# Routing in one 512-column product per block: the high and the low part of a transposed block side by side, their sum taken on VectorE

## The reference, cut to what matters

```python
W = weights[condition]                                   # 64 matrices of 128x128, chosen per batch
h = jnp.einsum('bct,bcd->bdt', x, W)                     # x is 64 x 128 x 2048
flat = h.reshape(T, H)                                   # one token: 2048 numbers
logits = jnp.einsum('th,eh->te', flat, router_weight) + router_bias     # 64 experts
scores = jax.nn.softmax(logits, axis=-1)
topk_w, topk_idx = jax.lax.top_k(scores, 8)
w_sum = topk_w.sum(axis=-1, keepdims=True)
bias_mix = jnp.einsum('te,eh->th', w_dense, expert_bias) # w_dense: topk_w at topk_idx, else 0
out = x + (flat * w_sum + bias_mix).reshape(...)
```

## Time and profile before

| | |
|---|---|
| median of 3 runs | 559.57 us (558.46 to 559.75) |
| the profiled execution | 558.69 us, of which its instructions span 556.9 us |
| TensorE busy | 541.0 us, 97% of the span |
| VectorE busy | 471.2 us, 85% |
| ScalarE busy | 368.5 us, 66% |
| GpSimd busy | 354.4 us, 64% |
| mean granted TensorE clock | 0.993 |

### The profile page before, as it was taken

How to read it: one execution, slowest core, us unless ns; L and a number is a source line. 1 busy time by engine, 2 the same in 40 slices (tenths; PEclk the granted TensorE clock), 3 DMA queues, 4 the chain that set the end, 5 groups by cost and what they waited for, 6 DMA issues and landing times.

```text
span 556.9 us, 12892 instructions
## 1 busy us (share of the span) xinstructions
PE 541.0 (97%) x3360; PEld 477.0 (86%) x3360; DVE 471.2 (85%) x1055; ACT 368.5 (66%) x836; POOL 354.4 (64%) x326
## 2 busy tenths in 40 slices
PE   5879999999999999999999999999999999999997
PEld 5768888888888888888888888888888888888875
DVE  2488898988889988889988889898888998888975
ACT  3576666677666677666677666667666667766661
POOL 0176666766666776666776666676666677666676
PEclk9979999999999999999999999999999999999999
DMA  8986999888999888898888999888899888889245
GB/s 243 311 201 231 309 297 279 292 300 287 297 318 276 269 311 289 295 325 280 292 276 296 294 311 300 271 290 297 286 298 315 284 283 295 288 294 326 119 166 212
DMA packets 70850, 155.96 MB, mean 280 GB/s; under 512 B 6322, under 2 KB 45234, under 8 KB 62770
## 3 DMA queue, kind: packets, MB, share of 16 engines
q1 hardware_dynamic: 70834, 155.77, 85.6%
HBM read 88.64 MB, written 67.11 MB: 280 GB/s over the span
## 4 chain that ended last, share of the span: by engine, by line
PE 93%; DMA 3%; SPq 1%; ACT 1%; issue 1%; DVE 1%; ACTq 0%; DVEq 0%
PE zt_ps L337 21%; PE xt_ps L325 14%; PE p_ps L390 11%; PE p_ps L387 11%; PE p_ps L385 11%; PE p_ps L386 10%; PE p_ps L391 10%; PE scores_ps L360 2%; DMA out_sb<-L_ffn_expert_bias 2%; PE scores_ps L369 1%; PE scores_ps L351 1%; DMA cond_sb<-itok_B 1%; SPq L243 0%; SPq L244 0%; DVE xt_lo L546 0%
## 5 line engine op out<-in xcount | busy, mean ns | idle before, releaser
L681 POOL TENSOR_TENSOR x_lo<-x_sb,x_hi 128x512 fp32r<-128x512 f32 x256 | 327.0, 1308 | 176.2 <-ACT x_hi L459 176.2
L546 DVE TENSOR_TENSOR xt_lo<-xt_ps,xt_hi 128x512 fp32r<-128x512 f32 x256 | 175.7, 687 | 63.6 <-ACT xt_hi L451 60.8
L451 ACT CAST xt_hi<-xt_ps 128x512 fp32r<-128x512 f32 x256 | 148.2, 582 | 102.9 <-PE xt_ps L325 84.9
L612 DVE SCALAR_TENSOR_TENSOR out_sb<-p_ps,w_sum,x_sb 128x512 f32<-128x512 f32 x256 | 189.6, 740 | 6.2 <-PE p_ps L391 6.2
L459 ACT CAST x_hi<-x_sb 128x1024 fp32r<-128x1024 f32 x128 | 133.7, 1045 | 0.5 <-PE p_ps L391 0.5
L337 PE MATMUL zt_ps<-xt_hi,router_hl 128*128 128x256 f32 x512 | 129.6, 285 | 4.5 <-DVE xt_lo L546 4.5
L337 PE MATMUL zt_ps<-xt_lo,router_hl 128*128 128x256 f32 x512 | 129.2, 285 | 0.0
L325 PE MATMUL xt_ps<-ident,x_sb 128*128 128x128 f32 x784 | 119.2, 277 | 0.1
L385 PE MATMUL p_ps<-x_hi,w_hl 128*128 128x512 f32 x256 | 118.8, 464 | 0.0
L337 PEld LDWEIGHTS zt_ps<-xt_hi,router_hl 128*128 128x128 f32 x512 | 98.1, 192 | 11.0 <-DVE xt_lo L546 5.2
L337 PEld LDWEIGHTS zt_ps<-xt_lo,router_hl 128*128 128x128 f32 x512 | 98.4, 192 | 4.8
(11 more groups left out here) (38 smaller groups left out, 368.7 us busy)
## 6 DMA issues: line engine op xcount, KB each, us to landing
out<-out_sb SPq DMA_DIRECT2D x126, 512.0 KB, 4.2
x_sb<-x SPq DMA_DIRECT2D x62, 1024.0 KB, 6.8
x_turn<-x SPq DMA_DIRECT2D x120, 128.0 KB, 4.7
w_sb<-L_cond_weights SPq DMA_DIRECT2D x64, 64.0 KB, 5.3
x_sb<-x SPq DMA_DIRECT2D x4, 256.0 KB, 6.0
x_sb<-x SPq DMA_DIRECT2D x2, 512.0 KB, 8.0
out_sb<-L_ffn_expert_bias SPq DMA_DIRECT2D x2, 512.0 KB, 9.4
out<-out_sb SPq DMA_DIRECT2D x4, 256.0 KB, 2.5
```

Of the source, the lines that this page charges most:

```text
L451: act.copy(xt_hi[:, n % 2, :, r, :], xt_ps[v % 4][:, :].rearrange("p (q c) -> p q c", c=P)).then_inc(xt_hi_ready, 1)
L546: dve.tensor_tensor(xt_lo[:, n % 2, :, r, :], xt_ps[v % 4][:, :].rearrange("p (q c) -> p q c", c=P), xt_hi[:, n % 2, :, r, :].bitcast(F32) ...
L612: dve.scalar_tensor_tensor(out_sb[:, r, cols], p_ps[n % 2][:, :], w_sum[:, o % 2, r:r + 1], x_sb[:, (2 * o + r) % XRING, cols], ALU.mult, ...
L681: pool.tensor_tensor(x_lo[:, r, cols], x_sb[:, (2 * o + r) % XRING, cols], x_hi[:, r, cols].bitcast(F32), ALU.subtract).then_inc(x_lo_read ...
```

## The change

`xt_hi` and `xt_lo` become one tile `xt_hl`, in which each block of 256 rounded columns is followed by its 256 columns of rests. `route` makes one product of 512 columns for each block, which fills the whole bank `zt_ps`: the sum over the rounded part stands in the first half, that over the rests in the second. ScalarE copies the first half to a new tile `zt_of_hi` in slot 1, and VectorE adds the second half to it (`zt_sum`, new, slot 1). `turn_z` moves from slot 1 to slot 2, and `z_sum` from slot 2 to slot 3. `score` stays where it was.

```diff
@@ route, TensorE
-                    for xt in (xt_hi, xt_lo):
-                        last = pe.matmul(zt_ps[:, 0:2 * P],
-                                         router_hl[:, t, :, :].rearrange("p a e -> p (a e)"),
-                                         xt[:, n % 2, q, :, :].rearrange("p r c -> p (r c)"),
-                                         start=(t == 0 and xt is xt_hi),
-                                         stop=(t == TB - 1 and xt is xt_lo))
+                    last = pe.matmul(zt_ps[:, :], router_hl[:, t, :, :].rearrange("p a e -> p (a e)"),
+                                     xt_hl[:, n % 2, q, :, :, :].rearrange("p h r c -> p (h r c)"),
+                                     start=(t == 0), stop=(t == TB - 1))
@@ step, TensorE
-                    if mid and v == 1:
+                    if mid and v == 2:
                         turn_z(m, i - 1)
@@ zt_copy, ScalarE
-                act.copy(zt_sb[:, :, :], zt_ps[:, 0:2 * P].rearrange("p (r c) -> p r c", r=2)).then_inc(zt_ready, 1)
+                wait(act, zt_ready, i)
+                act.copy(zt_of_hi[:, :, :],
+                         zt_ps[:, 0:2 * P].rearrange("p (r c) -> p r c", r=2)).then_inc(zt_of_hi_ready, 1)
@@ VectorE
+            def zt_sum(m, o):
+                i = 4 * m + o
+                dve.wait_ge(zt_of_hi_ready, i + 1)
+                dve.tensor_tensor(zt_sb[:, :, :], zt_ps[:, 2 * P:4 * P].rearrange("p (r c) -> p r c", r=2),
+                                  zt_of_hi[:, :, :], ALU.add).then_inc(zt_ready, 1)
@@ step, VectorE
-                    if mid and v == 2:
+                    if mid and v == 1:
+                        zt_sum(m, i - 1)
+                    if mid and v == 3:
                         z_sum(m, i - 1)
```

More of the change, by code:

```diff
@@ L90, in adaln_router @@
         w_hl = sb("w_hl", [P, 8, 2, D], F32R)
-        xt_hi = sb("xt_hi", [P, 2, BLOCKS, 2, P], F32R)
-        xt_lo = sb("xt_lo", [P, 2, BLOCKS, 2, P], F32R)
+        xt_hl = sb("xt_hl", [P, 2, BLOCKS, 2, 2, P], F32R)
         kept_t_hi = sb("kept_t_hi", [P, 2, 2, P], F32R)
@@ L97, in adaln_router @@
         w_sum = sb("w_sum", [P, 2, 2])
+        zt_of_hi = sb("zt_of_hi", [P, 2, P])
         zt_sb = sb("zt_sb", [P, 2, P])
@@ L158, in adaln_router @@
         w_hl_ready = sem("w_hl_ready")
+        zt_of_hi_ready = sem("zt_of_hi_ready")
         zt_ready = sem("zt_ready")
@@ L450, in xt_high @@
                 wait(act, routed, PIECES * i + n - 1)
-                act.copy(xt_hi[:, n % 2, :, r, :],
+                act.copy(xt_hl[:, n % 2, :, 0, r, :],
                          xt_ps[v % 4][:, :].rearrange("p (q c) -> p q c", c=P)).then_inc(xt_hi_ready, 1)
@@ L545, in xt_low @@
                 dve.wait_ge(xt_hi_ready, SLOTS * (4 * m + o) + v + 1)
-                dve.tensor_tensor(xt_lo[:, n % 2, :, r, :], xt_ps[v % 4][:, :].rearrange("p (q c) -> p q c", c=P),
-                                  xt_hi[:, n % 2, :, r, :].bitcast(F32), ALU.subtract).then_inc(xt_lo_ready, 1)
+                dve.tensor_tensor(xt_hl[:, n % 2, :, 1, r, :], xt_ps[v % 4][:, :].rearrange("p (q c) -> p q c", c=P),
+                                  xt_hl[:, n % 2, :, 0, r, :].bitcast(F32), ALU.subtract).then_inc(xt_lo_ready, 1)
             def relay(m, o, v):
```

## The result

| | before | after |
|---|---|---|
| median | 559.66 us (4 runs, 558.46 to 560.89) | 595.52 us (4 runs, 595.20 to 596.06) |
| ratio of the runs | 1 | 1.0642, 95% interval 1.0617 to 1.0666 |
| profiled execution | 558.69 us, span 556.9 | 595.20 us, span 593.3 |

The change makes the kernel 6.4% slower. The forecast was 592.1 us with a range of 585 to 598.

A forecast was written before the change was run, and what follows sets the result against it. TensorE, 97% busy, was taken as the bound. Each of 30 full steps loses 1.23 us at `score` less 0.11 gained, 33.6 us; remaining routing gives back 0.2, so 33.4 on 558.69 makes 592.1 us, range 585 to 598.

The forecast's parts named there:

- What bounds the kernel: Whole kernel: TensorE is full, busy 97% of the span; what one of 30 full steps gains or loses counts thirty times.
- The products: Routing on TensorE: 512-column products save 0.028 us a `route` call, 0.11 us a full step, 3.6 us in all.
- The addition: VectorE, slot 1: `zt_sum` pushes back what follows by 0.33 us, at most 0.41; TensorE doesn't wait for it at `turn_z`.
- z_sum and the wait at score: `z_sum` ends 1.58 us later against a margin of 0.54, so TensorE loses 1.23 us at `score` each full step.
- 0.06 us from the end of a VectorE operation to the product that it releases: Term of the loss at `score`: release delay of 0.06 us, read between `xt_low` and a product in the start.
- 0.10 us for the first product after a wait: Term of the loss at `score`: a first product after a wait takes 0.10 us more, 0.38 against 0.28.
- The start: Step 1: first scores may come about 1 us later, but a 3.61 us TensorE wait at 31.32 covers that.
- VectorE's addition costs the stretch nothing: Rival, VectorE's busy stretch: the addition fits into an unseen gap, 0.33 us leaves each wait, 582 us; chance 0.06.
- No wait: Rival at `score`: `z_sum` is in time, only the shorter routing is left, 555.1 us, faster; chance 0.05.
- The clock falls: Rival on TensorE: pauses each step lower its clock, costing 33 us, 625 us or more; chance 0.05, shared with another second wait.
- back-to-back issue gap: Skill page's rule for TensorE products, N/2.4 + 2.5 ns: products would gain 1.3 us, whole sum 2.3 us higher.

The follow-up runs named there:

- the first experiment: The changed kernel with `z_sum` alone put back to slot 2 on VectorE: 559.41 us, ratio 0.9991 to the kernel before.

## Why the prediction was right

**What bounds the kernel: right.** TensorE had no slack, and each wait in the loop came through in full; the table above has it at three delays.

**The products: right.** Forecast 0.028 us for a call of `route`, 0.11 us in a step and 3.6 us in all. Measured 0.13 us in a period and 3.6 to 4 us with the products alone.

**The addition: right.** 0.33 us from its start to the next one, 306.64 to 306.97. `turn_z` in slot 2 does not wait for it in the full steps.

**z_sum and the wait at score: right in place and nearly in size.** Forecast 1.23 us of loss at `score`, measured 1.30; three small terms were off. Shown by taking it away (one line moved back: 595.5 to 559.4) and by making it alone (1.0503 without products and addition). The term "0.06 us from the end of a VectorE operation to the product that it releases" was too small: it is 0.15 us at `score`, in each full step here and in all the kernels with a hold, and the missing 0.09 us is more than the 0.05 that the range allowed for distances. I had read it off a routing product; why that one starts sooner is not shown. The time doesn't go by the engine or the kind of product alone, as the last section has it. The term "0.10 us for the first product after a wait" is 0.08 here. The savings that stand against them were 0.13 and not 0.11. These misses partly cancel: +0.09, -0.02 and -0.02 make the 0.05 us by which the period, forecast as 17.65, is longer at 17.70.

**The start: wrong.** "TensorE waits 3.61 us a little behind them, which covers that" did not hold. Here are the waits of TensorE in the start of the changed kernel:

```profile
22.44 0.44 PE L349 MATMUL scores_ps<-ident,zt_sb 128*128 128x128 f32 x2 [1.25 <-DVE zt_sb L563]
25.18 0.86 PE L358 MATMUL scores_ps<-z_sb,w_sb 128*128 128x64 f32 x4 [1.82 <-DVE z_sb L569]
33.12 1.19 PE L337 MATMUL zt_ps<-xt_hl,router_hl 128*128 128x512 f32 x4 [2.04 <-DVE xt_hl L546]
36.87 0.50 PE L383 MATMUL p_ps<-x_hi,w_hl 128*128 128x512 f32 x1 [1.46 <-DVE expert_hl L642]
```

The cover was used, 2.04 us being left of 3.61, but what TensorE waited for there came 1.8 us later itself, at 33.12 for 31.32, and a wait for `expert_hl` followed it. One row of ScalarE in the same trace says that a part of this need not be the change's:

```profile
26.30 1.90 ACT L520 CAST expert_hl<-out_sb 128x2048 fp32r<-128x2048 f32 x1 [2.32 <-DMA out_sb<-L_ffn_expert_bias]
```

This copy waits for a transfer. It started at 25.15 in the profiled execution of before, and between 26.05 and 28.66 in the eight experiments, without any order by what they change. So this piece of the start differs by a microsecond or more between executions, and the sum was made against one in which it was early. The second `score` starts at 45.50 us, where it started at 43.02: 2.5 us later, of which the forecast hold of one full step is 1.2. So about 1.3 us of the 3 us between forecast and result stand in the first two steps. How much of that is the change's own is left open: in the first experiment, which lacks the hold, the second `score` starts at 44.66, already 1.6 us later than before, and with the products alone at 43.10. Another 1.5 us are the 0.05 us in each of the 29 steps that follow, and the rest, 0.2 us, lies in the last steps.

**The rivals.** "VectorE's addition costs the stretch nothing" fell: the stretch moved by the full 0.33 us. "No wait" fell, at the point where it was said to: the first experiment has only the 0.33 us in it, less than the margin, and `score` starts there without a wait, if with 0.06 us more for its passes. "The clock falls" fell: with 30 pauses of about 1.1 us it was 1.00 (2.4 GHz) from 40 to 570 us, the third number from the end of this row of the stretches.

```profile
40.00:570.00 530.00, 498.09 (x2631) 406.98 (x2630) 449.77 (x1019) 341.20 (x778) 329.88 (x302) 1.00 0.82 266
```

The page "TensorE: Matmul & The Clock Gate" of the Trainium skill, by whose back-to-back issue gap the products would gain 1.3 us, was further off than the rows of the projection, which gave 3.6. Measured are 3.6 to 4.

**What is not settled.** With `z_sum` in slot 2 and the addition on VectorE, the mean period is 16.50 and not 16.40. Some 0.06 of it is `score`'s start, shown above. The rest, about 0.04, shows as a later weight load of L388, for which `kept_t_lo` of VectorE is named: `kept_t_lo` ends 0.14 us ahead of its product on average there, against 0.41 with the products alone and 0.39 with the sum on GpSimd. That VectorE's addition as such is the cause is supported by the version without it, 16.39, but that version also has `turn_z` behind the routing, no run separates the two, and the path from the addition to `kept_t_lo` was not followed.

## What to carry to other kernels

An operation that is moved by one slot is moved past everything that its engine does in between, and on an in-order engine without idle time in that stretch the price is the sum of those operations less the margin to its consumer, and with it what the release and the restart of the waiting product take, 0.15 and 0.08 us here; read them off the timeline before moving. A gain on the full engine is small change against a wait on it: 0.13 us won in a step, 1.30 lost. And where a line waits for several semaphores, the profile's name for the wait, and the chain built on it, can be an accident of which came last, even of an increment that the wait did not need. Work out from the code which count the line waits for and when it was reached; moving the named writer is a cheap test.

## What was not expected of the hardware

- From the end of VectorE's `z_sum` to the start of `score`, an fp32 product, there are 0.14 to 0.15 us in every full step of the four kernels where it waits, and as many from the addition to `turn_z` in the kernel with `turn_z` back in slot 1; between `xt_low` and a routing product 0.05 to 0.06. That is no rule for fp32 products as such: the transposes of `turn_kept` started 0.05 us after ScalarE's `kept_twice` had ended. What makes the difference is not shown.
- Four passes of `score` ahead of transposes take 0.39 us when its input is there 0.54 us ahead, 0.43 when 0.18 ahead, and 0.47 (311.03 to 311.50) after a wait.
- Four transposes take 0.36 us ahead of a projection product and 0.44 ahead of an fp32 product. What stands behind a group of transposes decides 0.08 us of its time.
- The 128x256 addition takes 0.41 us on VectorE from PSUM and 0.74 on GpSimd from SBUF.
